# A graph network's ranking stage on one Trainium2 core: triangle mask by TensorE and ScalarE, count matrix two tiles at a time

## The chip, the cores and the metric

The kernel runs on one core of one Trainium2 chip. The metric is the device time of one execution in microseconds (us). The engines are TensorE (PE; its weight loads are shown apart as PEld), VectorE (DVE), ScalarE (ACT), GpSimd (POOL) and SyncE (SP, which only starts transfers).

## The reference

The reference runs four graph layers over the same 200,000 edges and 6,250 nodes. What matters here is what the edges are: `src` is random, `dst` is sorted and denser near node 0.

```python
src = jax.random.randint(jax.random.fold_in(_gk, 2), (200000,), 0, 6250, jnp.int32)
dst = jnp.minimum((6250 * jax.random.uniform(jax.random.fold_in(_gk, 3), (200000,)) ** 2.0).astype(jnp.int32), 49999)
_o = jnp.argsort(dst, stable=True)
src = src[_o]
dst = dst[_o]
...
x = x + _L0_gnn_ref(h, edge_index, edge_attr_32, ...)   # sum, max and mean of edge rows by src
x = x + _L1_gnn_ref(h, src, dst, ...)                   # sum of xn[src] by dst
x = x + _L2_gnn_ref(h, edge_index, edge_weight, ...)    # weighted sum of x[dst] by src
x = x + _L3_gnn_ref(h, edge_attr_64, src, dst, ...)     # two rounds of messages by dst
```

For the first and the third layer the kernel sorts the edges by `src`; for the second and the fourth it multiplies by a matrix that counts, for each pair (source, destination), how many edges join them.

## The kernel before, in words

One stage does both preparations: `rank_and_build`. It holds two unrelated pieces of work, laid into one another by hand in each engine's program.

**Ranking.** The edges stand as 1,568 columns of 128 (one edge in each partition), taken 8 at a time; 8 columns are a half turn `n`, two of them (`h` = 0 and 1) a turn `i`, and there are 98 turns. For a half turn DVE makes one-hot matrices of the source's low seven bits and of its high part (`oh_lo`, `oh_hi`, lines 248 and 249). PE turns `oh_lo` (line 557), ACT copies the result out twice (`lo_rows_b`, `lo_rows_f`, lines 505 and 506), and PE multiplies each turned column with itself (`compare`, line 566): `same` is 1 where two edges of the column have the same low bits. Of `same` only the part above the diagonal is wanted, the edges that come earlier: `mask` (line 428) multiplies it on DVE with the triangle of ones `belowb` and writes `earlier`. Then comes the serial `chain`: for each of 8 columns PE adds the column to the running counts (`running`, line 575), ACT copies the counts to the store (`counts`, line 524), and PE works out the rows (`count_rows`, lines 580 and 581). The next column's `running` waits for ACT's copy. After 8 columns DVE picks the places (`picked`, `place_i`, lines 434 and 440), and POOL sends the 8 columns of edge rows to their sorted places by indirect transfers (line 414). ACT also lays those rows together from the loaded attributes (lines 531 and 532).

**Count matrix.** The same edges in order of `dst` make 1,563 tiles of 128 edges. The matrix is built in 784 windows of 8 destinations. A window visits only the tiles that meet it, `WGRP` = 4 tiles to a group, and the number of groups of each window is worked out on the chip beforehand (`win_table`, line 864 on), so that both engines run a loop with a computed count. For each group DVE makes `window_keys` (line 460), the one-hot `low` (line 462) and the one-hot `high` (line 466), and PE adds `WGRP` products into `part` (line 595), after it has cleared the bank (line 589). Places beyond a window's own tiles are worked out all the same and find no match. There are two slots of `low` and `high`: DVE may be two groups ahead of PE and waits on `used`; PE waits on `made`. ACT copies a finished window into `slab` (line 510), and SP stores 16 windows at a time.

**The order.** A turn has 16 columns and 8 windows. PE does two columns of `chain`, then a window, and so on; the turning of the next half turn comes before column 2, and `compare` before column 7. DVE does a window before every second column, then at column 0 the picking and the one-hots of the next half turn, and at column 7 the mask. ACT does a counts copy at every column, the `lo_rows` copies at columns 3 and 5, at column 7 the rows (lines 531 and 532), and each window's copy one pair of columns later. At the start of a turn PE, DVE and ACT each load the bounds of its 8 windows from `win_table` into registers (`load_ranges`).

Of the kernel before, what the change touches and what calls it, by code (L numbers as in the profile page):

```python
# [7 lines left out]
BF16 = mybir.dt.bfloat16  # L8
FP16 = mybir.dt.float16
I32 = mybir.dt.int32  # L10
ACT = mybir.ActivationFunctionType
# [7 lines left out]
EP = 128  # L19
# [13 lines left out]
NWIN = 784  # L33
WGRP = 4
BLOCK_W = P // W
# [7 lines left out]
QUAD = 4  # L43
# [257 lines left out]
def rank_and_build(nc, g, edge_attr_32, sorted_rows, slabs):  # L301
# [13 lines left out]
    with Scope(nc) as s:  # L315
# [11 lines left out]
        high = s.sb("high", [EP, 2 * WGRP * KEYW], BF16)  # L327
        window_keys = s.sb("window_keys", [EP, 2 * WGRP], FP16)
        iota_g = s.sb("iota_g", [P, KEYW, 2], FP16)
        slab = s.sb("slab", [P, 2, HI, P], BF16)  # L330
# [9 lines left out]
        same_ready = s.sem("same_ready")  # L340
# [80 lines left out]
        def _(dve):  # L421
            def lo_hi(n, h):
                one_hots(nc, g, oh_lo[:, h], oh_hi[:, h], n).then_inc(oh_ready, 1)

            def mask(n, h):
                for q in range(2):
                    dve.wait_ge(same_ready, 2 * n + q + 1)
                    nc.vector.tensor_tensor(earlier[:, h, q], same[q][:, :].rearrange("p (u e) -> p u e", u=QUAD),
                                            g["belowb"][0:EP, 0:EP].unsqueeze(1).broadcast_to([EP, QUAD, EP]),
                                            ALU.mult).then_inc(earlier_ready, 1)  # L430

            def pick(n, h, before):
# [19 lines left out]
            def window(i, j, before, offset):  # L452
                base = g["winbase"][0:EP, bass.ds(i * WT + j, 1)]
                with dve.Fori(before[j], before[j + 1]) as v:
# [16 lines left out]
                                    KEY_SCALE, None, ALU.mult).then_inc(iota_ready, 1)  # L471
            dve.wait_ge(iota_ready, 1)
            dve.sem_inc(places_ready, 2)
            lo_hi(0, 0)
            mask(0, 0)
            def turn(i, since):
                before, offset = load_ranges(nc, g["win_table"], DVE, i * WT, WT, MOST)
                for h in range(2):
                    n = 2 * i + h
                    for u in range(RG):  # L480
                        if u % 2 == 0:
                            window(i, (h * RG + u) // 2, before, offset)
                        if u == 0:
# [5 lines left out]
                            lo_hi(n + 1, 1 - h)  # L489
                        if u == 7:  # L490
                            mask(n + 1, 1 - h)

# [7 lines left out]
        def _(act):  # L500
            act.sem_inc(rows_ready, 2)

            def lo_rows(n, h, q):
                act.wait_ge(turned_ready, n + 1)
                nc.scalar.copy(lo_rows_b[:, h, q], turned[:, q, :, 0:EP])
                nc.scalar.copy(lo_rows_f[:, h, q], turned[:, q, :, 0:EP]).then_inc(lo_rows_ready, 1)

            def window(k, m, j, before):
                act.wait_ge(used, before[j + 1] + 2)
                nc.scalar.copy(slab[:, k, :, bass.ds(m * (WT * W) + j * W, W)], part[j % 2][:, :, :]  # L510
                               ).then_inc(copied, 1)

            nc.scalar.copy(counts[:, 0, :], g["start"][:, 0:HI]).then_inc(counts_ready, 1)
            for q in range(2):
                lo_rows(0, 0, q)
            def turn(i, k, m, first):
                before, _ = load_ranges(nc, g["win_table"], ACTE, i * WT, WT, MOST)
                act.wait_ge(slab_free, i + 1)
                for h in range(2):
                    n = 2 * i + h  # L520
                    for u in range(RG):
# [3 lines left out]
                        if u in (3, 5):  # L525
                            lo_rows(n + 1, 1 - h, u // 4)
                        if u == 7:
                            act.wait_ge(attr_in[h], 32 * (i + 1))
                            if not first:
# [20 lines left out]
        def _(pe):  # L550
# [10 lines left out]
            def compare(n, h):  # L561
                for q in range(2):
                    pe.wait_ge(lo_rows_ready, 2 * n + q + 1)
                    for u in range(QUAD):
                        x = lo_rows_b[:, h, q, u, :]
                        last = nc.tensor.matmul(same[q][:, u * EP:(u + 1) * EP], x, x, start=True, stop=True)
                    last.then_inc(same_ready, 1)
# [34 lines left out]
            nc.tensor.matmul(running[:, :], g["ident"][:, :], g["start"][:, 0:HI], start=True, stop=True)  # L602
            turn(0, 0)
            compare(0, 0)
            with pe.Fori(0, NG // 2) as i:
# [166 lines left out]
def find_ranges(nc, g, scratch):  # L772
# [6 lines left out]
    with Scope(nc) as s:  # L779
# [47 lines left out]
        def _(dve):  # L827
# [38 lines left out]
            step(nc.vector.tensor_copy(steps_i[:, win], steps[:, win]))  # L866
            step(nc.vector.tensor_single_scalar(steps_i[:, win], steps_i[:, win], 2, ALU.arith_shift_right))
            step(nc.vector.tensor_copy(steps[:, win], steps_i[:, win]))
# [997 lines left out]
```

## Time and profile before

| what | us |
|---|---|
| median of 3 runs (lowest, highest) | 6668.84 (6654.18, 6673.85) |
| the profiled execution's own time | 6651.2 |
| its span | 6649.2 |
| PE busy | 3712.5 (56%) |
| DVE busy | 4112.3 (62%) |
| POOL busy | 3583.9 (54%) |
| ACT busy | 1237.5 (19%) |

The span is about 2 us shorter than the execution's own time. The shares are means over stages with different limits. The stage of this change lies from about 350 us to about 2826 us after the span's start, some 37% of it; what comes before are the keys and the ranges, what comes after are the scans, the gathers and the layers. Busy shares are to be read within that stage.

### The profile page before, as it was taken

Reading aid. Unit: us, or ns where it says so; the run is one execution under the profiler, and the core shown is the slowest. Engines: PE = TensorE matmul, PEld = TensorE weight load, DVE = VectorE, ACT = ScalarE, POOL = GpSimd, SP = SyncE. Lnnn points to the kernel's source line nnn. Section 1 sums busy time; section 2 is a strip of 40 time slices with the busy share of each in tenths; the row PEclk is TensorE's granted clock in tenths of the full one; section 3 lists DMA queues with packets and bytes.
Section 4 is the critical chain, followed back from the end, with each engine's and each line's share of the span. In section 5 each row is a group of like instructions: output and inputs, shape, how many; then the busy total and the mean of one; then the engine's idle time right before and its main releaser. Section 6 shows DMA issues by size and latency. Waiting matters only on the chain. (4 is left out here: it accounts for less than half of the span.)

```text
span 6649.2 us, 116495 instructions
## 1 busy us (share of the span) xinstructions
PE 3712.5 (56%) x27862; PEld 2888.6 (43%) x27863; DVE 4112.3 (62%) x11121; ACT 1237.5 (19%) x3929; POOL 3583.9 (54%) x3398
## 2 busy tenths in 40 slices
PE   4377777777787777800066875544322222127686
PEld 3234555555555555500055875544322222127474
DVE  8888877777777777779123777766544444221303
ACT  0023444444444444400000000000000000000101
POOL 0036777777777777600501777777777777620000
PEclk5599888888888878755587555555555555569898
DMA  0001121211112121166165444433332223238190
GB/s 24 2 20 47 51 62 51 61 52 55 58 51 62 51 61 52 50 225 259 35 288 208 103 96 99 100 85 85 74 70 65 65 62 67 50 141 345 65 409 10
DMA packets 459609, 634.35 MB, mean 95 GB/s; under 512 B 342019, under 2 KB 397479, under 8 KB 426087
## 3 DMA queue, kind: packets, MB, share of 16 engines
q1 hardware_dynamic: 347202, 493.86, 22.3%
q0 software_dynamic: 106624, 86.11, 6.3%
q10 hardware_dynamic: 5670, 53.26, 2.2%
q14 instruction: 90, 0.74, 0.0%
q8 instruction: 23, 0.38, 0.0%
HBM read 420.15 MB, written 212.81 MB: 95 GB/s over the span
## 5 line engine op out<-in xcount | busy, mean ns | idle before, releaser
L414 POOL DMA_INDIRECT sorted_rows<-rows,place_i x1568 | 1797.5, 1146 | 815.9 <-issue 463.7
L1349 POOL DMA_INDIRECT gathered_rows<-feature_table,gather_index x1568 | 1579.3, 1007 | 501.5 <-issue 463.0
L1435 PE MATMUL block_total<-attr_half,block_hot 128*128 128x65 f32 x4048 | 876.2, 418 | 320.0 <-DMA attr_half<-in_edge_attr_dram 312.7
L1435 PEld LDWEIGHTS block_total<-attr_half,block_hot 128*128 128x128 f32 x4048 | 867.2, 332 | 329.0 <-issue 309.7
L595 PE MATMUL part<-high,low 128*128 x3520 | 906.0, 387 | 124.7 <-DVE high L466 115.1
L466 DVE TENSOR_TENSOR high<-iota_g,window_keys 128x1568 f16 x880 | 850.5, 967 | 0.4
L580 PE MATMUL count_rows<-counts,lo_rows_f 128*128 128x49 f32 x3136 | 724.9, 323 | 0.0
L1393 DVE TENSOR_SCALAR block_hot<-iota_f,block_keys 128x128 f32<-128x128 f32 x2024 | 502.4, 302 | 183.7 <-PE block_total L1435 65.2
L580 PEld LDWEIGHTS count_rows<-counts,lo_rows_f 128*128 128x128 f32 x3136 | 585.5, 233 | 24.8 <-issue 19.7
L595 PEld LDWEIGHTS part<-high,low 128*128 x3520 | 378.1, 107 | 482.8 <-issue 344.1
L1404 DVE TENSOR_TENSOR_SCAN gathered_rows<-same_src,sum_carry,gathered_rows 128x32 f32<-128x32 f32 x3136 | 578.2, 264 | 6.2
L524 ACT COPY counts<-running 128x49 f32<-128x49 f32 x1568 | 315.1, 201 | 1368.2 <-PE running L575 1249.1
L1429 PE MATMUL block_total<-attr_rest,rest_hot 128*128 128x65 f32 x98 | 32.3, 433 | 883.6 <-DVE rest_hot L1380 851.0
L1399 DVE TENSOR_TENSOR gathered_rows<-gathered_rows,w_sorted 128x2048 f32<-128x2048 f32 x49 | 112.3, 2292 | 617.0 <-DMA gathered_rows<-feature_table,gather_index 615.5
L462 DVE TENSOR_TENSOR low<-iota_g,lo_tiles 128x512 f16 x880 | 486.5, 553 | 0.0
L575 PE MATMUL running<-oh_hi,oh_lo 128*128 128x49 bf16 x1568 | 321.8, 205 | 294.4 <-issue 219.8
L460 DVE TENSOR_SCALAR window_keys<-mkeys,winbase x880 | 204.4, 232 | 348.2 <-PE part L595 173.8
L1429 PEld LDWEIGHTS block_total<-attr_rest,rest_hot 128*128 128x128 f32 x98 | 24.5, 311 | 891.3 <-issue 891.3
L510 ACT CAST slab<-part 128x392 f32 (+1 forms) x784 | 392.5, 501 | 38.9 <-PE part L595 35.1
L1359 ACT COPY attr_sum<-block_total 128x65 f32 x49 | 10.5, 213 | 2085.7 <-PE block_total L1435 2085.7
L575 PEld LDWEIGHTS running<-oh_hi,oh_lo 128*128 128x128 bf16 x1568 | 170.1, 108 | 514.8 <-issue 400.7
L950 PE MATMUL sum_bank_round<-gated_parts,piece_round 128*128 128x129 f16 x4802 | 302.6, 222 | 97.2 <-DMA piece_round<-slabs 97.2
(352 smaller groups left out, 5522.5 us busy)
## 6 DMA issues: line engine op xcount, KB each, us to landing
piece_round<-slabs SPq DMA_DIRECT2D x98, 1568.0 KB, 23.0
slabs<-slab SPq DMA_DIRECT2D x49, 1568.0 KB
piece_conv<-slabs SPq DMA_DIRECT2D x49, 1568.0 KB, 23.0
attr_half<-in_edge_attr_dram SPq DMA_DIRECT2D x184, 352.0 KB
scanned<-scan_out ACTq DMA_DIRECT2D x8, 6272.0 KB, 30.4
scanned<-gathered_rows SPq DMA_DIRECT2D x49, 1024.0 KB, 5.1
scan_rows<-sorted_rows SPq DMA_DIRECT2D x8, 3430.0 KB, 30.3
sorted_rows<-rows,place_i POOLq DMA_INDIRECT x1568
```

Of the source, the lines that this page charges most:

```text
L414: pool.indirect_dma_start(sorted_rows[:, :], bass.IndirectOffsetOnAxis(ap=place_i[:, h, u:u + 1], axis=0), rows[:, h, u, :], None).then_in ...
L462: nc.vector.tensor_tensor(by_pairs(low[:, bass.ds(slot * (P * WGRP), P * WGRP)]), iota_pairs(P), pair_keys(g["lo_tiles"][:, bass.ds(t, WGR ...
L466: nc.vector.tensor_tensor(by_pairs(high[:, bass.ds(slot * (WGRP * KEYW), WGRP * KEYW)]), iota_pairs(KEYW), pair_keys(keys, KEYW), ALU.is_e ...
L510: nc.scalar.copy(slab[:, k, :, bass.ds(m * (WT * W) + j * W, W)], part[j % 2][:, :, :]).then_inc(copied, 1)
L524: nc.scalar.copy(counts[:, (u + 1) % 2, :], running[:, :]).then_inc(counts_ready, 1)
L575: nc.tensor.matmul(running[:, :], oh_lo[:, h, u // 2, :, u % 2], oh_hi[:, h, u // 2, :, u % 2], start=False, stop=True, skip_group_check=T ...
L580: nc.tensor.matmul(out, lo_rows_f[:, h, q, v, :], counts[:, u % 2, :], start=True, stop=False)
L595: last = nc.tensor.matmul(out, low[:, bass.DynSlice(slot * (P * WGRP) + q * 2 * P + b, P, 2)], high[:, bass.DynSlice(slot * (WGRP * KEYW) ...
L1349: pool.indirect_dma_start(got[b][:, j, :], None, table[:, :], bass.IndirectOffsetOnAxis(ap=index[b][:, j:j + 1], axis=0)).then_inc(gathere ...
L1393: nc.vector.tensor_scalar(hot[:, j, :], iota_f[0:EP, :], keys[:, j:j + 1], None, ALU.is_equal).then_inc(made, 1)
L1404: last = nc.vector.tensor_tensor_scan(got[b][:, :, f], g["same_src"][:, bass.ds(n * J, J)], got[b][:, :, f], carry[:, f:f + 1], ALU.mult, ...
L1435: nc.tensor.matmul(total[b][:, :], hot[:, j, :], attr[j // HALF][:, j % HALF, :], start=False, stop=True, skip_group_check=True).then_inc( ...
```

## The change

Two things are changed. The first: `WGRP` goes from 4 to 2, with the shift by which the number of groups is worked out. The second: the triangle is put on otherwise. `below_less_1`, made once, is 0 above the diagonal and -1 elsewhere; PE first writes it into all four columns of a `same` bank (a product of 512 columns with the identity), and adds the four products to it. Where two edges have the same low bits and the first comes earlier the sum is 1, elsewhere it is 0 or below. ACT then takes the maximum with zero (Relu) into `earlier`. So the mask leaves DVE's program for ACT's, and two products of 512 columns for each half turn come into PE's.

```diff
-WGRP = 4
+WGRP = 2
...
+        below_less_1 = s.sb("below_less_1", [EP, EP], BF16)
...
-            def mask(n, h):
-                for q in range(2):
-                    dve.wait_ge(same_ready, 2 * n + q + 1)
-                    nc.vector.tensor_tensor(earlier[:, h, q], same[q][:, :].rearrange("p (u e) -> p u e", u=QUAD),
-                                            g["belowb"][0:EP, 0:EP].unsqueeze(1).broadcast_to([EP, QUAD, EP]),
-                                            ALU.mult).then_inc(earlier_ready, 1)
-
...
+            def mask(n, h):
+                for q in range(2):
+                    act.wait_ge(same_ready, 2 * n + q + 1)
+                    nc.scalar.activation(earlier[:, h, q], same[q][:, :].rearrange("p (u e) -> p u e", u=QUAD), ACT.Relu
+                                         ).then_inc(earlier_ready, 1)
...
                         if u == 7:
+                            mask(n + 1, 1 - h)
                             act.wait_ge(attr_in[h], 32 * (i + 1))
...
                     pe.wait_ge(lo_rows_ready, 2 * n + q + 1)
+                    nc.tensor.matmul(same[q][:, :], g["identb"][:, :],
+                                     below_less_1[:, :].unsqueeze(1).broadcast_to([EP, QUAD, EP]), start=True, stop=True)
                     for u in range(QUAD):
                         x = lo_rows_b[:, h, q, u, :]
-                        last = nc.tensor.matmul(same[q][:, u * EP:(u + 1) * EP], x, x, start=True, stop=True)
+                        last = nc.tensor.matmul(same[q][:, u * EP:(u + 1) * EP], x, x, start=False, stop=True,
+                                                skip_group_check=True)
...
-            step(nc.vector.tensor_single_scalar(steps_i[:, win], steps_i[:, win], 2, ALU.arith_shift_right))
+            step(nc.vector.tensor_single_scalar(steps_i[:, win], steps_i[:, win], 1, ALU.arith_shift_right))
```

ACT's program around the end of a turn, from the last counts copies of a half turn (`counts`) over the rows and two windows (`slab`) to the next turn's loading of the bounds. Before:

```order
L524 COPY counts<-running 128x49 x2
L531 COPY rows<-attr 128x8x32
L532 COPY rows<-sdw 128x8x3
L509 REGISTER_ALU x2
L510 CAST slab<-part 128x49x8
L509 REGISTER_ALU x2
L510 CAST slab<-part 128x49x8
L901 TENSOR_LOAD win_table
```

And now:

```order
L523 COPY counts<-running 128x49 x2
L503 ACTIVATE earlier<-same 128x512 x2
L531 COPY rows<-attr 128x8x32
L532 COPY rows<-sdw 128x8x3
L507 REGISTER_ALU x2
L508 CAST slab<-part 128x49x8
L507 REGISTER_ALU x2
L508 CAST slab<-part 128x49x8
L905 TENSOR_LOAD win_table
```

Two operations of 512 columns now stand between the counts copy of column 7 and the rows, the windows and the next load.

PE's program of `compare`, the second place. Before:

```order
L566 MATMUL same<-lo_rows_b 128x128 x4
```

And now, with the added product first:

```order
L564 MATMUL same<-below_less,identb 128x512
L568 MATMUL same<-lo_rows_b 128x128 x4
```

Both come twice for a half turn, ahead of `chain` of column 7. Nothing else moved on PE but that a group's loop now holds two products and not four.

## Rows read from the trace of the kernel before

**Rows 1.** Busy time by stretch: PE, PEld, DVE, ACT, POOL, granted clock, DMA share.

```profile
350.00:712.00 362.00, 269.49 (x1773) 158.61 (x1774) 318.81 (x623) 120.32 (x384) 189.39 (x164) 0.91 0.12 38
1200.00:1800.00 600.00, 478.43 (x3390) 319.16 (x3390) 463.42 (x896) 279.93 (x897) 465.77 (x400) 0.83 0.18 55
```

**Rows 2.** Waits, 350 to 2830 us: us in total, times, longest us.

```profile
POOL sorted_rows L414 <- DVE place_i L440: 352.2, 114, 150.6
DVE window_keys L460 <- PE part L595: 170.5, 165, 2.5
DVE earlier L428 <- PE same L566: 160.6, 171, 1.8
PE turned_lo L557 <- DVE oh_hi L249: 120.4, 143, 1.0
PE part L595 <- DVE high L466: 105.4, 188, 1.2
```

**Rows 3.** Groups by line and form, 350 to 2830 us: count, busy us, mean ns.

```profile
L414 POOL DMA_INDIRECT sorted_rows<-rows,place_i x1561 | 1790.8, 1147 | 813.7 <-issue 461.6 <-DVE place_i L440 352.2
L466 DVE TENSOR_TENSOR high<-iota_g,window_keys 128x1568 f16 x862 | 833.1, 966 | 0.4
...
L428 DVE TENSOR_TENSOR earlier<-same,belowb 128x512 bf16<-128x512 f32 x392 | 252.3, 685 | 163.6 <-PE same L566 160.6 <-issue 2.9
L506 ACT CAST lo_rows_f<-turned_lo 128x512 f32<-128x512 bf16 x391 | 236.9, 606 | 0.0
...
L249 DVE TENSOR_TENSOR oh_hi<-iota,hi 128x392 bf16<-128x392 f16 x195 | 69.2, 355 | 0.0
```

**Rows 4.** Timeline, middle of a turn: start us, us, engine, line.

```profile
1500.44 0.20 ACT L524 COPY counts<-running 128x49 f32<-128x49 f32 x1 [0.55 <-PE running L575]
...
1501.51 0.20 PE L575 MATMUL running<-oh_hi,oh_lo 128*128 128x49 bf16 x1
...
1501.74 0.20 ACT L524 COPY counts<-running 128x49 f32<-128x49 f32 x1 [0.24 <-PE running L575]
...
1503.35 0.87 PE L595 MATMUL part<-high,low 128*128 x4 [0.72 <-DVE high L466]
...
1505.18 0.62 PE L557 MATMUL turned_lo<-identb,oh_lo 128*128 128x128 bf16 x8 [0.96 <-DVE oh_hi L249]
```

**Rows 5.** Timeline, end of a turn and start of the next.

```profile
1510.24 0.61 PE L566 MATMUL same<-lo_rows_b 128*128 128x128 bf16 x8
...
1512.18 0.96 POOL L414 DMA_INDIRECT sorted_rows<-rows,place_i  x1 [0.30 <-issue]
...
1514.64 0.22 PE L575 MATMUL running<-oh_hi,oh_lo 128*128 128x49 bf16 x1 [2.65 <-issue]
...
1516.49 0.20 ACT L524 COPY counts<-running 128x49 f32<-128x49 f32 x1 [3.89 <-issue]
...
1517.60 1.51 PE L595 MATMUL part<-high,low 128*128 x4
```

**Rows 6.** Timeline of DVE and PEld, two groups of one window.

```profile
520.17 0.23 DVE L460 TENSOR_SCALAR window_keys<-mkeys,winbase  x1 [1.11 <-PE part L595]
...
521.54 0.22 DVE L460 TENSOR_SCALAR window_keys<-mkeys,winbase  x1
...
522.01 0.97 DVE L466 TENSOR_TENSOR high<-iota_g,window_keys 128x1568 f16 x1
522.29 0.56 PEld L595 LDWEIGHTS part<-high,low 128*128 x4 [0.24 <-issue]
...
523.56 0.55 PEld L595 LDWEIGHTS part<-high,low 128*128 x4 [0.71 <-issue]
```

**Rows 7.** Timeline of PE and PEld, two groups at the lower clock.

```profile
406.43 2.62 PE L595 MATMUL part<-high,low 128*128 x8
...
407.09 0.15 PEld L595 LDWEIGHTS part<-high,low 128*128 x1 [0.18 <-issue]
...
407.55 0.34 PEld L595 LDWEIGHTS part<-high,low 128*128 x2 [0.31 <-issue]
```

More of the change, by code:

```diff
@@ L471, in _ @@
                                     KEY_SCALE, None, ALU.mult).then_inc(iota_ready, 1)
-            dve.wait_ge(iota_ready, 1)
+            nc.vector.tensor_scalar(below_less_1[:, :], g["belowb"][:, :], -1.0, None, ALU.add).then_inc(iota_ready, 1)
+            dve.wait_ge(iota_ready, 2)
             dve.sem_inc(places_ready, 2)
             lo_hi(0, 0)
-            mask(0, 0)
             def turn(i, since):
@@ L489, in turn @@
                             lo_hi(n + 1, 1 - h)
-                        if u == 7:
-                            mask(n + 1, 1 - h)
             turn(0, 0)
@@ L515, in _ @@
                 lo_rows(0, 0, q)
+            mask(0, 0)
             def turn(i, k, m, first):
@@ L603, in _ @@
             turn(0, 0)
+            pe.wait_ge(iota_ready, 2)
             compare(0, 0)
```

## The prediction

> **What bounds the kernel now.** I first read busy time by stretch [rows 1], to see which engine fills the stage that changes. No engine does. In the first 362 us (turns 0 to 10, where node 0's neighbourhood makes long windows) DVE is busy for 319 us; in the body, here 600 us of it, PE and DVE share the lead with 478 and 463 us, and POOL has 466 us of instructions with a fixed gap after each. Next come the waits [rows 2]: PE waits for DVE's one-hots (120.4 us) and for groups (105.4 us), DVE waits for PE's free slot (170.5 us) and for `same` (160.6 us). So PE and DVE pace each other, and in a body where a turn takes 24.3 us (87 turns from 712 to 2826 us) each engine's relief counts only as far as the other one follows. POOL is close behind: 16 transfers at 1.147 us [rows 3] with 0.30 us between them [rows 5] make 23.2 us for a turn, and its long wait for places (352.2 us) includes one of 150.6 us at the start [rows 2]. The timelines show what PE does at the two seams of a turn. In the middle it starts turning only 0.96 us after it could, and the group before came 0.72 us late [rows 4]. At the start of a turn it stands for 2.65 us while bounds are loaded, then runs at half clock for a while: four products take 1.51 us there and 0.87 us elsewhere [rows 4, 5].
>
> **How many groups.** From the reference's draw, window and tile meet 2,341 times. By fours that makes 880 groups (the page counts 3,520 products, the same number); by twos it makes 1,323 groups and 2,646 products. 141 of the 443 extra groups fall in the first 11 turns. In the body's 696 windows, all of one group now, 394 keep one (of two tiles) and 302 get two.
>
> **The change, part by part, in us on PE's path.**
>
> (1) *874 fewer products.* Four products in 0.87 us with a first one of 0.387 mean 0.16 each; at half clock eight in 2.62 us mean 0.33 [rows 4, 7]. The mean granted clock of 0.83 [rows 1] means that about a third of the time is at half clock, so 0.22 us: -190.
>
> (2) *443 more returns of PE's loop.* Between the loads of two groups of one window PEld stands 0.71 us, though DVE had finished the second group's `high` at 522.98, 0.58 us before the load at 523.56 [rows 6]. So the return itself costs that; loads in line follow each other within 0.04 us (four of 0.107 in 0.56). At full clock an extra return therefore costs 0.67 us; at half clock, where the queue of slow products hides most of it, 0.31 less 0.18 [rows 7], or 0.13. Mixed by the clock (a fifth at half clock in the first 11 turns, a third after): 141 x 0.57 + 302 x 0.49 = +229. All at the one or the other: +58 to +297. By that figure alone this term would be some +48 and the sum would come out near no change; the row's 0.71 us holds the whole return, register steps and refilling too, and I go by the row.
>
> (3) *392 added products of 512 columns.* At 0.16 us for 392 columns one takes 0.21 us. `compare` stands ahead of column 7's chain and ran at full clock (eight products in 0.61 us [rows 5]), and nothing on PE can pass it: +82.
>
> (4) *The mask on ACT.* Its nearest row is a copy of 512 columns from the same memory, 0.606 us [rows 3]; two overlapping make about 0.96 us. They stand after column 7's counts copy, ahead of rows and window copy, and the next half turn's first counts copy is queued behind. In mid-turn ACT is ready just when PE asks (counts copy at 1501.74, `running` at 1501.51 [rows 4]); with 0.96 us more, PE's second column starts some 0.7 us late: 98 x 0.7 = +69. At a turn's start PE's 2.65 us load covers it in half of the turns; in the other half ACT is the late one already (3.89 us idle [rows 5]), and I take +0.1 and +0.3 us, together +18. Bounds: 0 and 196 x 0.96 = +188.
>
> (5) *DVE is relieved.* 392 masks of 0.685 us and their waits go (252.3 + 160.6 us [rows 3, 2]), and a group gets shorter: between 128x392 (0.355 us) and 128x1568 (0.966 us) [rows 3] the 128x784 `high` lies at 0.56 us. For DVE this is much; for PE only its waits on DVE can vanish, 225.8 us at most [rows 2]. I take the mid-turn ones, 0.96 + 0.35 us for 98 turns: -128. The rest stays, since in long windows groups of two reach PE about as fast as it takes them (DVE 0.96 us, PE 0.71 + 0.28), and with only two slots of half the work DVE can look ahead less far.
>
> (6) *POOL's floor.* The late turns, nearly all of one-group windows, would come down to some 22.2 us, below what POOL needs (23.2 now, 22.5 if it meets DVE's long operations less; alone a transfer takes 0.96 [rows 5]). For 41 turns: +30.
>
> The making of `below_less_1` and the changed shift come once, under 1 us. The transfers don't notice that ACT is later: the rows are laid 1 us later, but POOL asks for them only after the places of the next half turn, which come later still.
>
> **Sum:** -190 + 229 + 82 + 87 - 128 + 30 = +110. The profiled execution took 6651.2 us, the median of the runs is 6668.84, 17.6 above. So 6761 on the profile's scale and 6779 on the median's; I say **6780**, 1.7% slower. A change within 0.3% (20 us) couldn't be told from none.
>
> **The rivals.**
>
> *A. DVE is what bounds the body, and the change frees it* (faster). For it: DVE's waits on `same` and PE's on DVE's one-hots are large and vanish together. Then a turn falls from 24.3 us to POOL's pace, 23.2 us or, with POOL disturbed less, 22.5: 87 x 1.1 to 87 x 1.8, and some 20 us in the first turns: -115 to -175, or 6555 to 6495 on the median's scale. Against it: PE's waits on DVE, 225.8 us in 98 turns, are 2.3 us of a turn, so 22.0 us are PE's own path, loads and ACT, and terms 3 and 4 add 1.7 us to that. It decides if an extra return costs PE less than about 0.2 us and the mask on ACT hides.
>
> *B. The terms cancel* (no change). The returns cost what they do at half clock, +58 in place of +229, or the mask on ACT hides wholly: 6640 to 6700.
>
> *C. DVE's loop has a floor of its own* (slower still). The shortest step from one group's keys to the next in a window is 1.37 us [rows 6], and that is no longer than its operations; if registers and branch take as much, groups of two gain DVE nothing. The first 11 turns then take 325 x 1.37 + 11 x 6 = 511 us and not about 430: 6850 to 6900.
>
> *D. The change does less than it says*, for instance because the mask waits on ACT for the attributes. It stands ahead of that wait, so this is unlikely and I give it no chance of its own.
>
> **How the numbers follow.** The forecast (PE-bound, +40 to +200 by the ends of terms 2, 4 and 5) has 0.57, A 0.22, B 0.09, C 0.12. Faster: A's 0.22. Same: B's within its middle, 0.10. Slower: the rest, 0.68. The range runs from 6550, A's upper end, to 6900, C's; what is left out is most of A's time with a faster POOL and a little above.
>
> **What would show it.** In the new profile of the stage: 1,323 groups and 2,646 products; PE busy nearly as before, but its waits on `high` and `oh_hi` down to under 100 us together; a gap of about 0.7 us between the loads of two groups of a window; ACT's two Relu at about 0.6 us, and PE's wait for `counts` up by some 80 us; DVE at 65 to 70% of a turn in the body. Turns 11 to 35, where most windows have three or four tiles, should take 26 us or more, and the late ones 22 to 23. If turns in the early body don't get longer, the return on PE costs less than I think, and the prediction is wrong there; if ACT's counts copies are not late in mid-turn, term 4 is.

## The result, and the profile after

The change makes the kernel slower: 6838.78 us (6833.66 to 6843.19, 4 runs) against 6661.51 us (6649.39 to 6673.85, 4 runs) for the kernel before on the same chip. The ratio is 1.027, with a 95% interval from 1.024 to 1.029: 177 us, where the prediction had 111 to its median. The profiled execution has a span of 6831.7 us.

The costliest lines of the page of the changed kernel:

```profile
PE 3856.9 (56%) x27382; PEld 2906.6 (43%) x27383; DVE 3832.8 (56%) x12057; ACT 1399.6 (20%) x4323; POOL 3353.1 (49%) x3398
...
L598 PE MATMUL part<-high,low 128*128 x2646 | 866.8, 429 | 184.7 <-DVE high L460 145.1
L454 DVE TENSOR_SCALAR window_keys<-mkeys,winbase x1323 | 323.7, 245 | 942.2 <-PE part L598 654.1
```

So the counts are the forecast ones: 1,323 groups, 2,646 products. What stands out is the last line: DVE, ahead of a group's keys, was idle for 942.2 us, 654.1 of them for a slot (one of the two buffers of `low` and `high`) that PE had yet to free. Within the stage that wait was 170.5 us before [rows 2] and is 649.1 now.

Busy time by stretch (PE, PEld, DVE, ACT, POOL, granted clock, DMA share), the same two stretches as [rows 1], and the last part of the stage:

```profile
350.00:712.00 362.00, 253.75 (x1083) 125.82 (x1083) 232.41 (x678) 80.94 (x245) 89.94 (x92) 0.55 0.07 22
1200.00:1800.00 600.00, 479.00 (x3022) 297.60 (x3021) 395.81 (x1110) 288.24 (x889) 354.16 (x356) 0.77 0.16 50
2581.00:3000.00 419.00, 345.06 (x2462) 233.58 (x2461) 242.19 (x659) 250.00 (x785) 318.39 (x315) 0.82 0.21 64
```

In the first stretch all engines do less than before in the same 362 us: DVE falls from 319 to 232 us, POOL from 189 to 90 us, and the granted clock from 0.91 to 0.55, where 0.5 would be the level of 1.2 GHz throughout. No engine is full and all do less, which fits two engines that wait for each other in turn.

The waits of the stage, 350 to 3010 us, to be held against [rows 2]:

```profile
POOL sorted_rows L415 <- DVE place_i L434: 758.1, 131, 180.9
DVE window_keys L454 <- PE part L598: 649.1, 510, 3.9
DVE window_keys L454 <- issue: 279.1, 600, 2.5
PE part L598 <- DVE high L460: 135.4, 204, 1.5
PE running L578 <- ACT counts L523: 106.5, 173, 3.6
PE turned_lo L557 <- DVE oh_hi L249: 69.9, 78, 1.3
```

PE's waits on DVE are 205.3 us in all, of 225.8 before. They didn't vanish: those on `oh_hi` fell by 50.5 us, those on `high` rose by 30. PE's wait for `counts` was 51.1 us in the trace before, so it rose by 55.

Where the time went can be read from the turns. ACT copies `rows` twice in a turn; here are the copies that end turns 0, 10 and 34 of the changed kernel (start us, us):

```profile
430.60 0.42 ACT L531 COPY rows<-attr 128x256 f32<-128x256 f32 x1
...
878.93 0.42 ACT L531 COPY rows<-attr 128x256 f32<-128x256 f32 x1
...
1578.95 0.42 ACT L531 COPY rows<-attr 128x256 f32<-128x256 f32 x1
```

In the kernel before, the same copies start at 391.46, 712.35 and 1292.06 us. Mean us for one turn, from such copies, and the difference over the whole stretch:

| turns | before | after | difference |
|---|---|---|---|
| to the end of turn 0 | | | +39 |
| 1 to 10 (long windows) | 32.1 | 44.8 | +127 |
| 11 to 34 | 24.2 | 29.2 | +120 |
| 35 to 56 | 24.3 | 24.3 | +2 |
| 57 to 79 | 24.4 | 22.0 | -54 |
| 80 to 97 | 24.4 | 21.3 | -55 |

The stage as a whole is 179 us longer. (Its first product on PE starts at 310.89 us in this trace and at 309.76 us in the one before, so the stage begins some 40 us earlier than the 350 us read ahead of the change, and turn 0 with it.) So the change is two things at once: it loses 286 us in the first 35 turns and gains 109 in the last 41. By the number of groups in a turn's eight windows the changed kernel's body needs 20.9 us for 8 groups, 22.1 for 10, 23.8 for 11, 26.6 for 14 and 30.2 for 16: from 11 to 16 groups each one costs (30.2 - 23.8) / 5 = 1.28 us.

What these 1.28 us are can be seen in a long window. Timeline of PE, PEld and DVE in the changed kernel (start us, us, engine, line; in brackets the idle time before):

```profile
443.16 0.83 PE L598 MATMUL part<-high,low 128*128 x2 [0.95 <-DVE high L460]
443.18 0.23 DVE L454 TENSOR_SCALAR window_keys<-mkeys,winbase  x1 [0.28 <-issue]
...
443.55 0.57 DVE L460 TENSOR_TENSOR high<-iota_g,window_keys 128x784 f16 x1
...
444.38 0.83 PE L598 MATMUL part<-high,low 128*128 x2 [0.39 <-DVE high L460]
444.42 0.23 DVE L454 TENSOR_SCALAR window_keys<-mkeys,winbase  x1 [0.31 <-issue]
...
444.80 0.57 DVE L460 TENSOR_TENSOR high<-iota_g,window_keys 128x784 f16 x1
...
445.63 0.83 PE L598 MATMUL part<-high,low 128*128 x2 [0.41 <-DVE high L460]
445.65 0.23 DVE L454 TENSOR_SCALAR window_keys<-mkeys,winbase  x1 [0.28 <-issue]
```

Keys follow keys after 1.24 us: 0.94 us from the start of the keys to the end of `high`, then 0.3 us in which DVE waited for nothing that the trace shows. That is where its loop's return lies (the end of one pass and the start of the next); an experiment below prices it. PE starts each group 0.26 us after its `high` ends and has stood idle for 0.4 us by then. Within this window DVE sets the pace, and it makes two tiles in 1.24 us where it made four in 1.37 at its fastest [rows 6].

### The profile page after: what moved, and what is told of

It reads as the page before. It is cut to its first block and busy times, and to the rows that moved or that the text cites. A ratio compares the mean times of both kernels' runs of the same rounds, so it can differ in the third digit from the quotient of the medians.

```text
span 6831.7 us, 122194 instructions
## 1 busy us (share of the span) xinstructions
PE 3856.9 (56%) x27382; PEld 2906.6 (43%) x27383; DVE 3832.8 (56%) x12057; ACT 1399.6 (20%) x4323; POOL 3353.1 (49%) x3398
## 5 line engine op out<-in xcount | busy, mean ns | idle before, releaser
L415 POOL DMA_INDIRECT sorted_rows<-rows,place_i x1568 | 1567.1, 999 | 1225.8 <-DVE place_i L434 758.1
L598 PE MATMUL part<-high,low 128*128 x2646 | 866.8, 429 | 184.7 <-DVE high L460 145.1
L454 DVE TENSOR_SCALAR window_keys<-mkeys,winbase x1323 | 323.7, 245 | 942.2 <-PE part L598 654.1
L583 PE MATMUL count_rows<-counts,lo_rows_f 128*128 128x49 f32 x3136 | 770.9, 342 | 0.0
L460 DVE TENSOR_TENSOR high<-iota_g,window_keys 128x784 f16 x1323 | 745.6, 564 | 4.6
L583 PEld LDWEIGHTS count_rows<-counts,lo_rows_f 128*128 128x128 f32 x3136 | 635.0, 251 | 16.9 <-issue 7.7
L598 PEld LDWEIGHTS part<-high,low 128*128 x2646 | 283.2, 107 | 606.5 <-issue 529.3
L456 DVE TENSOR_TENSOR low<-iota_g,lo_tiles 128x256 f16 x1323 | 472.3, 357 | 1.6
```

The source lines that it names most:

```text
L415: pool.indirect_dma_start(sorted_rows[:, :], bass.IndirectOffsetOnAxis(ap=place_i[:, h, u:u + 1], axis=0), rows[:, h, u, :], None).then_in ...
L454: nc.vector.tensor_scalar(keys, g["mkeys"][:, bass.ds(t, WGRP)], base, KEY_SCALE, ALU.subtract, ALU.mult).then_inc(keys_ready, 1)
L456: nc.vector.tensor_tensor(by_pairs(low[:, bass.ds(slot * (P * WGRP), P * WGRP)]), iota_pairs(P), pair_keys(g["lo_tiles"][:, bass.ds(t, WGR ...
L460: nc.vector.tensor_tensor(by_pairs(high[:, bass.ds(slot * (WGRP * KEYW), WGRP * KEYW)]), iota_pairs(KEYW), pair_keys(keys, KEYW), ALU.is_e ...
L583: nc.tensor.matmul(out, lo_rows_f[:, h, q, v, :], counts[:, u % 2, :], start=True, stop=False)
L598: last = nc.tensor.matmul(out, low[:, bass.DynSlice(slot * (P * WGRP) + q * 2 * P + b, P, 2)], high[:, bass.DynSlice(slot * (WGRP * KEYW) ...
```

## The experiments

All twelve are variants of the kernel before or of the changed one, and each was timed beside the kernel before. Differences are between medians; the ratios carry 95% intervals. Times of single turns come from one trace each. In the expectations, theory P says that PE's path paces the stage, theory D that DVE does in the long windows.

### The two parts apart

The first has the groups of two alone, on the kernel before, with its mask on DVE:

```diff
-WGRP = 4
+WGRP = 2
...
-            step(nc.vector.tensor_single_scalar(steps_i[:, win], steps_i[:, win], 2, ALU.arith_shift_right))
+            step(nc.vector.tensor_single_scalar(steps_i[:, win], steps_i[:, win], 1, ALU.arith_shift_right))
```

> Groups of two tiles, the mask left on VectorE. Theory P (TensorE's path paces the stage, an extra loop return costs it 0.5 to 0.7 us): the two-tile part carries nearly all of the loss, and with the mask still on VectorE its waits stay; about 6800 to 6850 us. Theory D (VectorE paces the long windows: in the changed kernel's trace its groups of a window follow each other in 1.27 to 1.35 us though their operations take about 1.0, with 0.2 to 0.35 us shown as issue): VectorE has the mask on top, so this is slower than the full change, 6850 to 6950 us, and the first eleven turns are longer still.

Measured: 6935.23 us against 6664.15, ratio 1.041 (1.039 to 1.043), +271 us. That is theory D's range and above theory P's. The prediction's terms 1, 2 and 6 give +69 for it.

The second is the change with `WGRP` left at 4 and the shift at 2, so that only the mask moves.

> Groups of four tiles as before, mask by TensorE addition and ScalarE maximum. Theory P: +82 us for the added products and +87 us for ScalarE's delay, less up to 128 us of waits that vanish: 6670 to 6710 us. Theory D (VectorE is the pace-setter of the first turns and half of the body): relief of 1.3 us and more for each half turn, so faster, 6450 to 6600 us.

Measured: 6615.54 us, ratio 0.993 (0.991 to 0.995), -49 us. This lies between the two theories' ranges. The prediction's terms 3, 4 and 5 give +41. Each part was missed, in opposite directions. The parts add up to +222 and the change is +177, so they are not independent. Where they meet can be read from the copies of `rows` in the three traces (us, against the trace before):

| turns | two tiles alone | mask alone | both |
|---|---|---|---|
| 0 to 34 | +281 | -15 | +287 |
| 35 to 56 | +35 | -9 | +2 |
| 57 to 97 | -33 | -10 | -109 |

In the first 35 turns, where the loss is, groups of two cost nearly the same whether the mask is DVE's or not. In the last 41 the parts gain 33 and 10 us alone and 109 together: with the mask alone a turn there stays at POOL's pace (worked out below), and with groups of two alone POOL's transfers are short (0.984 us in the mean) but a turn still takes 23.4 to 23.7 us, more than POOL needs.

Why the kernel with the mask alone gains no more is in its waits and in its POOL line (waits, 350 to 2830 us):

```profile
DVE window_keys L454 <- PE part L598: 468.2, 342, 4.8
...
PE running L578 <- ACT counts L523: 255.7, 175, 5.7
...
ACT rows L531 <- DMA sorted_rows<-rows,place_i: 100.4, 63, 3.2
```

And its groups of instructions (count, busy us, mean ns, idle before):

```profile
L415 POOL DMA_INDIRECT sorted_rows<-rows,place_i x1568 | 1849.2, 1179 | 734.3 <-issue 477.1 <-DVE place_i L434 257.3
```

A turn of its body needs 23.6 to 24.2 us, and 16 transfers of 1.179 us with 477.1 / 1,507 = 0.32 us of issue between them need 24.0. POOL's wait for places is down to 257.3 us, 147.5 of it at the start. So POOL is at its limit in most of that body: ACT now waits for the scattered rows to leave `rows` (100.4 us), a wait of 1.8 us in the trace before, and PE waits for ACT in turn (255.7 us, of 51.1 before).

### What a return costs, on each engine

PE's return by itself: the kernel before with DVE's groups left as they are, and PE taking each in two passes of two products, 880 returns more.

```diff
-                with pe.Fori(before[j], before[j + 1]) as v:
-                    slot = v & 1
+                with pe.Fori(before[j] * 2, before[j + 1] * 2) as v:
+                    slot = v & 3
                     pe.wait_ge(made, v + 1)
-                    for k in range(WGRP):
+                    for b in range(2):
...
-                        pair_keys(keys, KEYW), ALU.is_equal).then_inc(made, 1)
+                        pair_keys(keys, KEYW), ALU.is_equal).then_inc(made, 2)
```

> The kernel before, but TensorE's loop takes each group of four as two passes of two products: 880 more returns on TensorE, the same 3520 products, VectorE untouched. Theory P: 880 x 0.49 = 430 us less what hides behind the waits on VectorE (at most 226 us): 200 to 430 us slower. Theory D: in the long windows VectorE needs 1.65 us for four tiles and TensorE has room for one more return; under 200 us slower.

Measured: 7193.68 us, ratio 1.081 (1.079 to 1.083), +530 us, or 0.60 us for each of the 880. That is above both theories' ranges; the prediction had 0.49 to 0.57. The stretches of the body come to 28.6 to 28.8 us a turn, so the price is the same early and late in it. The 0.60 us hold all that a further pass brings: the return, a wait on `made` and a signal on `used`. The Trainium skill's page "Advanced Engine Details and Errata", section Control Flow Timing, puts a compare-and-branch at about 108 ns. An estimate from that figure alone would be 95 us for 880 passes; a pass costs over five times as much here, and no run shows the branch by itself.

DVE's return by itself: PE untouched, DVE makes each group of four in two passes of two tiles, with the four half-size slots that the same memory gives. DVE's look-ahead, eight tiles, stays.

```diff
-                with dve.Fori(before[j], before[j + 1]) as v:
-                    t = nc.s_assert_within(v * WGRP - offset[j], 0, DT, skip_runtime_bounds_check_because=RANGES)
-                    slot = v & 1
+                with dve.Fori(before[j] * 2, before[j + 1] * 2) as v:
+                    t = nc.s_assert_within(v * 2 - offset[j], 0, DT + 2, skip_runtime_bounds_check_because=RANGES)
+                    slot = v & 3
...
-                    pe.wait_ge(made, v + 1)
+                    pe.wait_ge(made, v * 2 + 2)
...
-                    last.then_inc(used, 1)
+                    last.then_inc(used, 2)
```

> The kernel before, but VectorE makes each group of four as two passes of its loop, two tiles each: 880 more returns on VectorE, TensorE untouched. If VectorE's step is only its operations (0.96 us for two tiles, against 1.6 for four) that is 0.3 us for each group of four, 280 us of VectorE time, about half of it hidden: 50 to 200 us slower (theory P). If a return has a floor of 1.3 us (theory D), it is 0.9 to 1.0 us for each group: 300 to 750 us slower.

Measured: 7280.26 us, ratio 1.093 (1.091 to 1.095), +616 us, 0.70 us for each extra pass. DVE's passes cost more than PE's. But this price has two parts, the return and the fixed cost of smaller operations; the next kernel takes the return away and keeps the operations, with both passes in one loop body:

```diff
-                with dve.Fori(before[j] * 2, before[j + 1] * 2) as v:
+                with dve.Fori(before[j], before[j + 1]) as w:
+                  for part_ in range(2):
+                    v = w * 2 + part_
```

> As the run with VectorE's doubled returns (7280 us), but both passes of two tiles stand in one loop body: the same 1760 operations of each kind, 880 returns fewer. If the return itself has a price on VectorE (steps of 1.28 us where the operations take 0.95), half or more of the 616 us goes: 6850 to 7000 us. If the two-tile operations' fixed time is what costs, less than 100 us goes: 7180 to 7280 us.

Measured: 6904.72 us against 6662.8, ratio 1.036 (1.034 to 1.038), +242 us. So some 376 of the 616 us are returns, 0.43 us each, and 242 are the smaller operations, 0.27 us for each added pass. Of the same line, the keys, first in the kernel with two passes:

```profile
L460 DVE TENSOR_SCALAR window_keys<-mkeys,winbase x1760 | 463.3, 263 | 716.8 <-issue 575.0 <-PE part L595 141.8
```

and in the one with both in one body:

```profile
L462 DVE TENSOR_SCALAR window_keys<-mkeys,winbase x1760 | 485.1, 276 | 341.6 <-issue 323.9 <-PE part L597 17.0
```

The idle time by "issue" falls by 251 us, and the wait for PE's slots with it.

### Look-ahead

In the changed kernel two slots hold four tiles where they held eight. This kernel is the change with four slots, so eight tiles again:

```diff
-        low = s.sb("low", [EP, 2 * P * WGRP], BF16)
-        high = s.sb("high", [EP, 2 * WGRP * KEYW], BF16)
-        window_keys = s.sb("window_keys", [EP, 2 * WGRP], FP16)
+        low = s.sb("low", [EP, 4 * P * WGRP], BF16)
+        high = s.sb("high", [EP, 4 * WGRP * KEYW], BF16)
+        window_keys = s.sb("window_keys", [EP, 4 * WGRP], FP16)
...
-                    slot = v & 1
+                    slot = v & 3
...
-                act.wait_ge(used, before[j + 1] + 2)
+                act.wait_ge(used, before[j + 1] + 4)
...
-            pe.sem_inc(used, 2)
+            pe.sem_inc(used, 4)
```

> The changed kernel with four slots of low and high, so that VectorE may be four groups of two ahead (as many tiles as before the change). If the shallower look-ahead is what costs, VectorE's 600 us of waits for TensorE's free slot shrink and some 50 to 100 us come back: 6740 to 6790 us. If only the returns cost, no change within 0.3%: 6820 to 6860 us.

Measured: 6658.52 us (10 runs) against 6662.8 (13 runs), ratio 0.9995 (0.9985 to 1.0004). All of the change's loss is gone, 180 us and far more than the 50 to 100 expected, with the 443 extra returns still in both engines' loops. Its waits:

```profile
DVE window_keys L454 <- PE part L598: 200.2, 284, 2.5
...
PE part L598 <- DVE high L460: 70.8, 151, 0.8
```

DVE's wait for a slot fell from 649.1 to 200.2 us and PE's for `high` from 135.4 to 70.8. The run shows the price; the mechanism that fits its waits is this. While PE does the rest of a turn (`chain`, turning, `compare`, the load of the bounds), DVE can make only what the slots hold. With four tiles in them it stands early, PE finds them used up soon, and then waits for each group at DVE's 1.24 us. With eight it comes to that later. The two stretches of [rows 1] in this kernel:

```profile
350.00:712.00 362.00, 281.11 (x1381) 147.14 (x1381) 281.58 (x817) 108.93 (x330) 122.34 (x126) 0.68 0.10 30
1200.00:1800.00 600.00, 476.09 (x3312) 293.33 (x3311) 415.55 (x1160) 319.70 (x991) 391.26 (x398) 0.87 0.18 55
```

Turns 1 to 10 come down from 44.8 to 36.7 us, 11 to 34 from 29.2 to 26.3, and the late ones only from 21.3 to 20.9. They aren't back at the 32.1 and 24.2 us before; the returns are still there.

Is it the number of slots or the work in them (the look-ahead, counted in tiles)? The kernel before with four slots (of four tiles; the edit is the same):

> The kernel before with four slots, so VectorE may be sixteen tiles ahead and not eight. If what the change lost was look-ahead counted in tiles, eight were enough and this gains little: 6600 to 6670 us. If the number of slots matters whatever the group, it gains as much as in the changed kernel (180 us): 6450 to 6520 us.

Measured: 6628.77 us against 6662.34, ratio 0.996 (0.994 to 0.997), -34 us. On this kernel the doubling from eight tiles to sixteen brings a fifth of what the one from four to eight brings on the changed kernel. Its waits show one reason (350 to 2830 us):

```profile
DVE earlier L428 <- PE same L566: 340.0, 184, 5.0
...
DVE window_keys L460 <- PE part L595: 6.5, 7, 1.4
```

The wait for slots is gone, 170.5 to 6.5 us, and the mask's wait for `same` took it over, 160.6 to 340.0. With the mask on DVE a longer look-ahead ends at the mask. With the new mask more than eight tiles still help: in the first 35 turns, in groups of four, four slots (the run with the switch at turn 35, below) take 58 us less than two (the mask alone), where the kernel before gains 26 us there.

### The granted clock

In the first stretch the granted clock fell to 0.55. Is this what makes the turns long, or does it only show that PE waits? This kernel adds one product of zeros, 392 columns, ahead of each wait for a group, 1,323 in all:

```diff
                     slot = v & 1
+                    nc.tensor.matmul(out, g["zerob"][0:EP, 0:P], g["zerob"][0:EP, 0:KEYW], start=False, stop=True,
+                                     skip_group_check=True)
                     pe.wait_ge(made, v + 1)
```

> The changed kernel, with one more product of zeros by zeros (392 columns) in TensorE's loop ahead of the wait for each group: 1323 products that change nothing in the sum. If the lower granted clock of the long windows (0.56 against 0.90 before) costs time, the product raises the clock there and the first eleven turns get shorter, by 20 to 80 us, while the late turns lose 1323 x 0.16 at most; in all between 6750 and 6850 us. If the clock is only a symptom, the first turns stay as they are, since VectorE paces them, and the rest pays for the products: 6900 to 7050 us.

Measured: 6810.0 us, ratio 1.022 (1.020 to 1.024), 29 us less than the change although PE does more.

```profile
350.00:712.00 362.00, 270.81 (x1426) 128.84 (x1425) 252.08 (x730) 92.00 (x278) 104.95 (x104) 0.89 0.08 24
1200.00:1800.00 600.00, 489.85 (x3339) 292.05 (x3337) 394.58 (x1097) 290.63 (x898) 358.45 (x359) 0.90 0.16 50
```

The granted clock is back at 0.89 and 0.90, and turns 1 to 10 take 41.9 us instead of 44.8. The added products cost PE some time of their own, so 2.9 of the 12.7 us that a turn had lost is the least that the clock is worth there; if the 24 products of a turn were all on PE's path at 0.16 us each (an estimate from term 1's price), it would be 2.9 + 3.9 = 6.8. The turns still take 9.8 us more than before at nearly the same granted clock (0.91 before), so the low clock is a part of the loss, and not the whole: it is also a sign that PE waits.

### ACT's two maxima in one place

Term 4 had them delay PE's second column. Here the second of the two stands after column 1 of the next half turn, where its reader (column 4) is still far:

```diff
-            def mask(n, h):
-                for q in range(2):
+            def mask(n, h, q):
...
+                        if u == 1:
+                            mask(n, h, 1)
                         if u == 7:
-                            mask(n + 1, 1 - h)
+                            mask(n + 1, 1 - h, 0)
```

> The changed kernel with ScalarE's second maximum moved from column 7 to column 1 of the next half turn, where it isn't needed until column 4. If ScalarE's 0.96 us at the seam is on the path, about half of it comes back: 196 x 0.3 = 60 us at most, 6780 to 6810 us. If it is hidden in the long turns and in the late ones behind GpSimd, nothing within 0.3%: 6820 to 6860 us.

Measured: 6850.48 us, ratio 1.029 (1.027 to 1.031), 12 us more than the change and not less. But the delay wasn't taken away, it was moved. It is plain in the changed kernel, here around a half turn's end (start us, us, engine, line):

```profile
1961.20 0.20 PE L578 MATMUL running<-oh_hi,oh_lo 128*128 128x49 bf16 x1
...
1962.22 0.23 ACT L523 COPY counts<-running 128x49 f32<-128x49 f32 x1
...
1962.50 0.20 PE L578 MATMUL running<-oh_hi,oh_lo 128*128 128x49 bf16 x1 [0.84 <-ACT counts L523]
```

PE's second column starts 1.30 us after its first. In the mean of the 98 mid-turns this distance is 0.49 us before, 1.05 us in the changed kernel and 0.67 us here; at the starts of turns it is 1.12, 0.95 and 1.29 us. What the move gave in mid-turn it took at the turn's start, and PE's wait for `counts` hardly fell (99.8 us from 106.5). So the run doesn't show whether the delay is on the path.

### Groups of a size by place

The turns say that groups of four are right early and groups of two late. The next three have both: DVE's and PE's loops over the turns are split at a turn `SPLIT`, and the tables of groups are made by fours ahead of it and by twos behind. The core of it:

```diff
-WGRP = 2
+WGRP = 4
+SPLIT = 49
...
-            with dve.Fori(2, NG // 2) as i:
+            with dve.Fori(2, SPLIT) as i:
                 turn(i, 2)
+            with dve.Fori(SPLIT, NG // 2) as i:
+                turn(i, 2, 2)
...
-            with pe.Fori(0, NG // 2) as i:
+            for first, end, size in ((0, SPLIT, 4), (SPLIT, NG // 2, 2)):
+              with pe.Fori(first, end) as i:
...
+            parts = ((slice(0, SPLIT * WT), 4, 2), (slice(SPLIT * WT, NWIN), 2, 1))
+            for some, size, shift in parts:
+                step(nc.vector.tensor_scalar(steps[:, some], steps[:, some], float(size - 1), None, ALU.add))
```

The mask is the new one. First with two slots and the switch at turn 49:

> Mask by TensorE and ScalarE; windows of the first 49 turns in groups of four tiles, those of the last 49 in groups of two. By the turns of the two runs at hand: as the run with the mask alone up to turn 49 (6615 us in all), then 24.1 us less about 2.1 for turns 57 to 79, 2.8 for turns 80 to 97 and 0.5 for 49 to 56: 100 us less, 6500 to 6530 us. If the turns don't carry over because GpSimd bounds them (1.18 us for each transfer with long VectorE operations, 1.00 with short ones), the gain is the same only if its transfers get short again; otherwise 6590 to 6620 us.

Measured: 6535.33 us against 6662.8, ratio 0.981 (0.979 to 0.982), -127 us, 5 us above the expected range. Turns 80 to 97 take 21.0 us, turns 1 to 10 take 31.8.

Then with four slots, and the switch at turn 35:

> Mixed groups and four slots together: groups of four tiles up to turn 35, of two from there, new mask. From the turns of the runs at hand (23.7 us up to turn 35 with the mask alone, 23.5, 21.8 and 20.9 us after it with four slots): 6510 to 6530 us. If deeper look-ahead also helps the groups of four, less: down to 6470 us.

Measured: 6475.0 us (6463.06 to 6478.81) against 6662.34, ratio 0.972 (0.970 to 0.973), -187 us. Turns 35 to 56, now by twos, took 24.5 us, and turns 11 to 34, by fours, 22.8 us. (Turns 35 to 56 took 23.5 us in the changed kernel with four slots, also by twos; this difference of 1 us isn't explained.) So the switch seemed too early; the last one moves it to turn 57.

> Mixed groups with four slots, the switch to groups of two at turn 57 in place of 35. In the run with the switch at 35, turns 35 to 56 (11.7 groups of two for 8 windows) took 24.5 us each, and turns 11 to 34 in groups of four 22.8. If groups of four hold 22.8 in turns 35 to 56 too, 22 x 1.7 = 37 us less than 6475: 6430 to 6450 us. If one window in two with an extra return costs no more than what groups of four cost there, the same as before the move, 6465 to 6485 us.

Measured: 6440.14 us (6429.25 to 6451.31) against 6661.39, ratio 0.967 (0.965 to 0.969), -221 us, as expected if groups of four hold their pace. This is the fastest of all. Turns 35 to 56 take 23.0 us and 80 to 97 take 20.7. The stretches of [rows 1] in it:

```profile
350.00:712.00 362.00, 296.88 (x2062) 176.27 (x2061) 315.06 (x632) 162.97 (x499) 222.06 (x192) 0.95 0.15 45
1200.00:1800.00 600.00, 486.45 (x3628) 315.22 (x3629) 410.54 (x859) 337.25 (x1044) 465.61 (x423) 0.90 0.20 61
```

PE gets through more instructions in either stretch than in any kernel above, at a granted clock of 0.95 and 0.90.

## Why the prediction was right, and where it was not

The sign and the range held: 6780 us forecast, 6838.78 measured. The mechanism held in part only. The likeliest case, PE's path with a bounded cost for each term, gives the time, but in long windows DVE sets the pace and in the last turns POOL does. And that the number came so near was luck: the sum was 66 us short of the measured difference, the remainder of larger misses. The two-tile part was forecast at +69 and came to +271 alone (202 too low); the mask was forecast at +41 and came to -49 alone (90 too high); and together they cost 45 less than apart.

**How many groups, and where.** Right: 1,323 groups and 2,646 products. That the price lies early and the gain late was in the text, and the turns show it.

**Term 1, fewer products (-190), and term 2, returns of PE's loop (+229).** Their prices held, as far as they could be tried. A further pass came to 0.60 us on PE, for 0.49 to 0.57. And where look-ahead is as before, the two-tile part costs what they say: the change with four slots, less the kernel with the mask alone, is 6658.5 - 6615.5 = +43, against +39 by the two terms. (Eight tiles fit the slots of both kernels; what differs is the size of a group.) By place it fits too: the two terms give +141 us for turns 0 to 34 (376 groups of four, 693 of two) and -105 for the rest, and the two traces lie +138 and -121 apart. The late agreement is partly chance, for with the mask alone those turns stand at POOL's pace, and its transfers got shorter with the groups of two. In the late turns the gap of 0.71 us is hardly paid, for with 8.4 to 9.6 groups in eight windows PE takes few extra returns. One side sum of the text is wrong: with 48 us for the returns in place of 229 it would give 110 - 229 + 48 = -71 us, a faster kernel, and not one "near no change".

**The step that failed: look-ahead, in term 5.** The text said that groups of two "reach PE about as fast as it takes them", and that with two slots of half the work DVE "can look ahead less far", and gave the second no price. It is as large as term 1 or term 2. Four slots in place of two take 180 us off the changed kernel. PE's waits on DVE, counted as 128 us saved, fell by 20.5 only, because those on `high` rose as those on `oh_hi` fell; the bound that the text set for them (under 100 us together) was broken by 205.3.

**Rival C was half right.** It said that DVE's loop has a floor of its own, at 1.37 us for a group. The floor is there, at 1.24 us, with the 0.3 us of return in it, and a return on DVE costs the kernel before 0.43 us. By this floor alone the first 11 turns' 325 groups would be 325 x 1.24 = 403 us. They took 568 us (from the stage's first product at 310.89 us to the end of turn 10 at 878.93), so some 165 us, 15 a turn, are time in which DVE wasn't making groups. Its waits for a slot are 114.4 us of that, and its picking and one-hots are busy for 47 us (groups of instructions, 310.8 to 879 us):

```profile
L454 DVE TENSOR_SCALAR window_keys<-mkeys,winbase x325 | 76.7, 236 | 197.3 <-PE part L598 114.4 <-issue 82.7
```

That is the other half: full slots, and a rest of the turn beside which nothing more could be made. The rival's own sum, 511 us, allowed 6 us a turn for it.

**Term 3, the added products (+82), and term 4, the mask on ACT (+87).** One operation of each kind costs about what was said. The changed kernel's rows:

```profile
L503 ACT ACTIVATE earlier<-same 128x512 bf16<-128x512 f32 x392 | 214.0, 600 | 0.0
...
L564 PE MATMUL same<-below_less,identb 128*128 128x512 bf16 x392 | 187.9, 479 | 0.0
```

A maximum takes 0.600 us, forecast 0.606. A product is recorded with 0.479 us, but the records of successive products overlap; what it holds PE up is the distance to the next product's start:

```profile
1959.69 0.38 PE L564 MATMUL same<-below_less,identb 128*128 128x512 bf16 x1
1959.90 0.39 PE L568 MATMUL same<-lo_rows_b 128*128 128x128 bf16 x4
```

That is 0.21 us, as reckoned; in the mean of all it is 0.30 us in the changed kernel, where part of them ran at the lower clock, so 117 us for the 392 and not 82. Term 4's delay is there as well: PE's second column in mid-turn came 0.56 us later in the mean, forecast 0.7, and its wait for `counts` rose by 55 us, forecast 80. At the starts of turns, where the text took +18 us, the second column came no later (0.95 us after the first, 1.12 before). How much of either term lies on the path isn't shown. With the mask alone the whole kernel gained 49 us, so DVE's relief, term 5, is worth 49 us more than terms 3 and 4 together, whatever these cost. The text had put it 41 us below them.

**Term 6, POOL's floor (+30).** Too high. It rested on 22.5 us a turn, and the late turns take 21.3. The changed kernel's row:

```profile
L415 POOL DMA_INDIRECT sorted_rows<-rows,place_i x1560 | 1559.4, 1000 | 1223.4 <-DVE place_i L434 758.1 <-issue 457.9 <-ACT rows L532 7.4
```

With 1.000 us and 457.9 / 1,417 = 0.32 us of issue between them, 16 transfers need 21.1 us. That is the pace of turns 80 to 97, and turns 57 to 79 come near it (22.0): together they gain the 109 us.

**Rival A** (DVE bounds the body, and the change frees it) holds for the late 41 turns: they fell to or near POOL's pace, as it says. It fails for the early ones, where the change burdens DVE instead: three operations and a return for two tiles.

**The signs that were named.** Turns 11 to 35 at 26 us or more: 29.2 for 11 to 34. Late ones at 22 to 23: 22.0 and 21.3. PE's waits on `high` and `oh_hi` under 100 us together: 205.3. DVE at 65 to 70% in the body: 395.81 of 600 us, 66%. A gap of 0.7 us between the loads of two groups: there where `high` is ready (0.71 us in the late turns), but 0.96 to 0.99 us in the long window shown above, since DVE is late.

**Left open.** The old mask with groups of two and four slots was not run, so how look-ahead and the mask's place work together is known for groups of four alone. Nor was it tried how much of the added products and of ACT's delay is on the path.

## What to carry to other kernels

A smaller group pays a loop return on every engine that walks the groups, not only on the one that looks like the bound (0.60 us for each on PE and 0.43 us on DVE, each tried alone on the kernel before). When a unit of work is halved, the buffers between two engines hold half the time as well: count look-ahead in work, and raise the number of slots with the change. And where the load is uneven, read the time by place before taking one size for all: the same change lost 286 us early and won 109 us late, and with each size in its own place, four slots and the new mask the kernel became 221 us faster than the one before. Last, a change of two parts wants a run of each: here both were misjudged, and their sum hid it.

## What the runs showed of the hardware

**POOL's transfers get shorter with DVE's operations.** The mean of an indirect transfer for the scattered rows was 1.147 us before [rows 3], 1.000 us after and 1.179 us with the mask alone. By overlap in the traces, a transfer beside a `high` of 1,568 elements took 1.212 us in the mean and one beside none 1.005 us in the kernel before; beside a `high` of 784 elements it took 1.017 us in the changed one, and 0.958 us beside none. With no DVE operation beside it at all a transfer took 0.957 to 0.958 us in both. With the groups of two alone, the mask still on DVE, the mean was 0.984 us. So where the mask is done isn't what shortens them; the size of DVE's operation goes with it. Why was not settled.

**Busy for nothing, and faster.** 1,323 products of zeros put the granted clock of the first stretch from 0.55 to 0.89 and took 29 us off the changed kernel.
